# Sixteen-head attention of a two-layer decoder: on even quads the shifted scores are transposed before the exponential, and the norm's last scaling is done by GpSimd

## The reference, cut to what matters

```python
x = _layernorm(x + _L1_attn_ref(x, ...))           # 16 heads, band mask
x = _layernorm(x + _L1_xattn_ref(x, ctx, ctx, ...)) # 16 heads, no mask

scores = einsum('bhqd,bhkd->bhqk', qh, kh) * scale  # 16 heads of 16
attn = softmax(scores, axis=-1)
out = einsum('bhqk,bhkd->bhqd', attn, vh)
concat = out.transpose(0, 2, 1, 3).reshape(B, LQ, D_MODEL)
return concat @ Wo + bo
```

## Time and profile before

| | us |
|---|---|
| median of 3 runs | 1810.71 |
| lowest, highest | 1802.79, 1812.08 |
| the profiled execution | 1797.77 |
| its span, first to last instruction | 1795.9 |

### The profile page before, as it was taken

How to read it: one execution, slowest core, us unless ns; L and a number is a source line. 1 busy time by engine, 2 the same in 40 slices (tenths; PEclk the granted TensorE clock), 3 DMA queues, 4 the chain that set the end, 5 groups by cost and what they waited for, 6 DMA issues and landing times.

```text
span 1795.9 us, 28713 instructions
## 1 busy us (share of the span) xinstructions
PE 1699.1 (95%) x10847; PEld 1507.1 (84%) x10896; DVE 1058.9 (59%) x2330; ACT 624.3 (35%) x1459; POOL 113.1 (6%) x105
## 2 busy tenths in 40 slices
PE   6999999998999999989999879999998999999997
PEld 5888888887989998977777669999998888989896
DVE  6766676675555544575555456677676364444446
ACT  0312222132222222212222245566665334444443
POOL 1000000000000000020000023111111000000001
PEclk9999999998999999989999979999898899999999
DMA  5000000101111111100000185565662000010001
GB/s 200 1 22 4 13 12 12 35 1 46 36 34 36 34 35 33 33 9 18 13 29 0 17 117 67 73 81 78 100 85 46 25 12 25 13 29 18 23 23 47
DMA packets 43778, 68.98 MB, mean 38 GB/s; under 512 B 4640, under 2 KB 33568, under 8 KB 43552
## 3 DMA queue, kind: packets, MB, share of 16 engines
q1 hardware_dynamic: 43680, 67.71, 19.1%
HBM read 36.24 MB, written 2.10 MB: 21 GB/s over the span
## 4 chain that ended last, share of the span: by engine, by line
PE 85%; DVE 9%; issue 3%; ACT 1%; DMA 1%; SPq 1%; DVEq 0%; POOL 0%; POOLq 0%; ACTq 0%
PE ps L111 22%; PE ps L112 21%; PE ps L113 21%; PE ps L1591 6%; PE ps L411 3%; PE ps L1578 3%; PE ps L430 2%; PE ps L1568 2%; PE ps L419 1%; PE ps L440 1%; PE ps L1117 1%; DVE X L917 1%; SPq L1426 1%; DVE a1PT L617 1%; PE ps L1601 1%
## 5 line engine op out<-in xcount | busy, mean ns | idle before, releaser
L898 DVE TENSOR_TENSOR m6hT_l<-m6h,m6hT_h 128x512 fp32r<-128x512 f32 x128 | 88.8, 694 | 189.8 <-ACT m6hT_h L804 189.6
L900 DVE SCALAR_TENSOR_TENSOR m2hT_l<-ps,m2hT_h 128x512 fp32r<-128x512 f32 x128 | 88.5, 691 | 157.5 <-ACT m2hT_h L806 157.5
L806 ACT ACTIVATE m2hT_h<-ps 128x512 fp32r<-128x512 f32 x128 | 76.4, 597 | 282.4 <-PE ps L113 282.4
L1673 ACT ACTIVATE nPr<-ps,negm 128x128 f32<-128x128 f32 x512 | 145.7, 370 | 66.4 <-DVE negm L1755 66.2
L803 ACT ACTIVATE m6h<-ps,m6b 128x512 f32<-128x512 f32 x128 | 88.2, 689 | 220.0 <-PE ps L113 205.3
L495 ACT ACTIVATE a1Pr<-ps,negm 128x128 f32<-128x128 f32 x256 | 73.0, 368 | 259.8 <-DVE negm L559 259.8
L111 PE MATMUL ps<-w_h,m6hT_h 128*128 128x256 f32 x512 | 145.4, 284 | 1.4 <-DVE X L917 0.8
L112 PE MATMUL ps<-w_l,m6hT_h 128*128 128x256 f32 x512 | 145.7, 285 | 0.0
L113 PE MATMUL ps<-w_h,m6hT_l 128*128 128x256 f32 x512 | 145.7, 284 | 0.0
L1755 DVE TENSOR_REDUCE negm<-ps 128x4 f32<-128x512 f32 x128 | 88.0, 688 | 97.4 <-PE ps L1568 97.3
L113 PE MATMUL ps<-m2w_h,m2hT_l 128*128 128x256 f32 x512 | 145.0, 283 | 0.0
(11 more groups left out here) (270 smaller groups left out, 4286.5 us busy)
## 6 DMA issues: line engine op xcount, KB each, us to landing
nKm<-nKc_h SPq DMA_DIRECT2D x64, 128.0 KB, 4.5
nQs<-nQc_h SPq DMA_DIRECT2D x64, 128.0 KB, 6.7
raw<-in_w_e1i SPq DMA_DIRECT2D x9, 512.0 KB, 3.5
raw<-in_w_e1o SPq DMA_DIRECT2D x9, 512.0 KB, 3.7
raw<-in_w_e6i SPq DMA_DIRECT2D x9, 512.0 KB, 3.6
raw<-in_w_e6o SPq DMA_DIRECT2D x9, 512.0 KB, 3.6
raw<-in_w_a SPq DMA_DIRECT2D x8, 512.0 KB, 4.2
nKm<-nKc_l SPq DMA_DIRECT2D x32, 128.0 KB, 5.2
```

The source lines that it names most:

```text
L806: nc.scalar.activation(c.hT[0][:, ch, :], ps[:, u % 2, :], ACT.Relu).then_inc(c.s["hi_ready"], 1)
L898: last = nc.vector.tensor_tensor(c.hT[1][:, ch, :], c.h32[:, u % 2, :], c.hT[0][:, ch, :].bitcast(F32), ALU.subtract)
L900: last = nc.vector.scalar_tensor_tensor(c.hT[1][:, ch, :], ps[:, u % 2, :], 0.0, c.hT[0][:, ch, :].bitcast(F32), ALU.max, ALU.subtract)
L1673: last = nc.scalar.activation(N.Pr[:, i % 4, j, :], ps[:, SB[i % 2], j * S:(j + 1) * S], ACT.Exp, bias=negm[:, i % 4, j:j + 1])
```

## The change

On even quads VectorE, as soon as it has the negated maximum, adds it to the four heads' scores in one instruction (`negm` broadcast along each head) and writes the result to `nPr`, signalling `p_even`. TensorE transposes these shifted scores, and ScalarE takes the exponential of the transposed bank in one instruction of 512 columns. On odd quads the exponential stays where it was (signal `p_odd`), and ScalarE copies the transposed bank as before. So ScalarE takes every transposed bank back to SBUF, and VectorE none; `pt_even` and `pt_odd` become one `pt_ready`. The normalised `X` is written by GpSimd right behind its power, and not by VectorE two steps later; the residual sum of sequence B waits until the `X` of sequence B - 2 is written. `following` comes after all of VectorE's steps.

```diff
     def pt_ready(n):
-        return N.s["pt_odd" if n % 2 else "pt_even"], n // 2 + 1
+    def p_ready(n):
+        return N.s["p_odd" if n % 2 else "p_even"], n // 2 + 1
...
-            steps += [(kind, (n - at) // 4) for kind, at in (("zn", 6), ("na", 9), ("ns", 9), ("nb", 11))
+            steps += [(kind, (n - at) // 4) for kind, at in (("zn", 6), ("na", 9), ("ns", 9))
...
                 nc.gpsimd.tensor_tensor(rstd[:, b:b + 1], veps[:, b:b + 1], mhalf[:, b:b + 1],
                                         ALU.pow).then_inc(s["rstd_ready"], 1)
+                pool.wait_ge(s["rstd_ready"], i + 1)
+                nc.gpsimd.tensor_scalar(X[:, i % B, :], N.r[:, i % 2, :], mv[:, b, 0:1], rstd[:, b:b + 1],
+                                        ALU.subtract, ALU.mult).then_inc(s["x_done"], 1)
...
             if n >= 2:
-                pe.wait_ge(s["p_ready"], n - 1)
+                pe.wait_ge(*p_ready(n - 2))
...
         def transpose_p(n):
-            pe.wait_ge(s["p_ready"], n + 1)
+            pe.wait_ge(*p_ready(n))
             if n > 1:
-                pe.wait_ge(*pt_ready(n - 2))
+                pe.wait_ge(s["pt_ready"], n - 1)
...
         def transposed_p(n):
             act.wait_ge(s["pt_full"], n + 1)
             nc.scalar.activation(N.PT[:, n % 2, :, :].rearrange("p a b -> p (a b)"), ps[:, TB[n % 2], :],
-                                 ACT.Identity).then_inc(s["pt_odd"], 1)
+                                 ACT.Identity if n % 2 else ACT.Exp).then_inc(s["pt_ready"], 1)
...
             elif kind == "s":
-                if i >= 2 and i % 2:
+                if i >= 2:
                     transposed_p(i - 2)
-                act.wait_ge(s["s_max"], i + 1)
-                for j in range(QH):
-                    last = nc.scalar.activation(N.Pr[:, i % 4, j, :], ps[:, SB[i % 2], j * S:(j + 1) * S], ACT.Exp,
-                                                bias=negm[:, i % 4, j:j + 1])
-                last.then_inc(s["p_ready"], 1)
+                if i % 2:
+                    act.wait_ge(s["s_max"], i + 1)
+                    for j in range(QH):
+                        last = nc.scalar.activation(N.Pr[:, i % 4, j, :], ps[:, SB[i % 2], j * S:(j + 1) * S], ACT.Exp,
+                                                    bias=negm[:, i % 4, j:j + 1])
+                    last.then_inc(s["p_odd"], 1)
...
         def norm_a(B):
+            if B >= 2:
+                v.wait_ge(s["x_done"], B - 1)
...
                 nc.vector.reduce_max(negm[:, i % 4, :], ps[:, SB[i % 2], :].rearrange("p (h k) -> p h k", h=QH), AX.X,
                                      negate=True).then_inc(s["s_max"], 1)
-            elif kind == "t":
                 if i % 2 == 0:
-                    v.wait_ge(s["pt_full"], i + 1)
-                    nc.vector.tensor_copy(N.PT[:, i % 2, :, :].rearrange("p a b -> p (a b)"), ps[:, TB[i % 2], :]).then_inc(s["pt_even"], 1)
+                    v.wait_ge(s["s_max"], i + 1)
+                    nc.vector.tensor_tensor(N.Pr[:, i % 4, :, :], ps[:, SB[i % 2], :].rearrange("p (h k) -> p h k", h=QH),
+                                            negm[:, i % 4, :].unsqueeze(2).broadcast_to([P, QH, S]), ALU.add).then_inc(s["p_even"], 1)
...
-            elif kind == "nb":
-                if i == NSEQS - 1:
-                    following()
-                norm_b(i)
+        following()
```

More of the change, by code:

```diff
@@ L1368, in program @@
     N.V, N.Km, N.Qs, N.XB = n_V, n_Km, n_Qs, n_XB
-    N.s = signals("n", "g_full g_evac xt_hi qk_hi ct_hi ct_ready ctx_loaded s_full s_max p_ready pt_full pt_even pt_odd z_full "
+    N.s = signals("n", "g_full g_evac xt_hi qk_hi ct_hi ct_ready ctx_loaded s_full s_max p_even p_odd pt_full pt_ready z_full "
                        "rec_done z_ready zt_full zt_hi zt_ready o_full r_done xb_ready ln_var rstd_ready x_done")
@@ L1372, in program @@
     N.k_laid = [sem(f"n_k_laid{j}") for j in range(2)]
-    def pt_ready(n):
-        return N.s["pt_odd" if n % 2 else "pt_even"], n // 2 + 1
+    def p_ready(n):
+        return N.s["p_odd" if n % 2 else "p_even"], n // 2 + 1
     SB = (0, 1)
@@ L1395, in n_order @@
             step = [("s", n), ("t", n - 2), ("pv", n - 3)]
-            step += [(kind, (n - at) // 4) for kind, at in (("zn", 6), ("zt", 7), ("o", 8), ("na", 8), ("ns", 9), ("nb", 10))
+            step += [(kind, (n - at) // 4) for kind, at in (("zn", 6), ("zt", 7), ("o", 8), ("na", 8), ("ns", 9))
                      if (n - at) % 4 == 0]
@@ L1587, in values @@
                     pe.wait_ge(s["z_ready"], n // 4)
-            pe.wait_ge(*pt_ready(n))
+            pe.wait_ge(s["pt_ready"], n + 1)
             for i in range(QH):
@@ L1665, in n_scalar @@
             elif kind == "t":
-                if i >= NQUADS - 2 and i % 2:
+                if i >= NQUADS - 2:
                     transposed_p(i)
             elif kind == "s":
-                if i >= 2 and i % 2:
+                if i >= 2:
                     transposed_p(i - 2)
-                act.wait_ge(s["s_max"], i + 1)
-                for j in range(QH):
-                    last = nc.scalar.activation(N.Pr[:, i % 4, j, :], ps[:, SB[i % 2], j * S:(j + 1) * S], ACT.Exp,
-                                                bias=negm[:, i % 4, j:j + 1])
-                last.then_inc(s["p_ready"], 1)
+                if i % 2:
[4 more added lines that the diff above has]
+                    last.then_inc(s["p_odd"], 1)
             elif kind == "zt":
@@ L1734, in norm_stats @@
             nc.vector.tensor_scalar(veps[:, b:b + 1], mv[:, b, 1:2], LN_EPS, None, ALU.add).then_inc(s["ln_var"], 1)
[L1736 to L1742, removed]
         for kind, i in n_order_vector():
```

## The result

The changed kernel takes 1855.22 us (median of 4 runs, 1846.89 to 1862.35), against 1811.07 for the kernel before: a ratio of 1.0252, 95% interval 1.0198 to 1.0307. That is 44 us slower, where 28 were forecast. The direction and the range held. The size did not hold in one term. Each kernel is measured beside runs of the kernel before on the same chip, and ratios and intervals leave out runs over 1.5% slower than the fastest of their kernel, which the medians keep.

The account below looks back on a forecast made before the run. TensorE, busy 95% of the span, was taken to bound the kernel. Output projection stops 17.8, longer `z_ready` stops 2.4 and lower clock 8 made 28 us, set on the median 1810.7: 1839 us, range 1820 to 1862.

Parts of the forecast that it names:

- Part 1: ScalarE's exponentials: one of 512 columns for four, taken as 600 ns, and the even copies; cost 0.
- Part 2: VectorE's subtraction ahead of `late`: `nzT_l` 0.71 us later, output projection stops 17.8 us, longer `z_ready` stops 2.4 us.
- The 2.4 us of that term: Chain to `z_ready` in step 4B+6: 0.12 us longer at each of 20 stops, bounds 0 and 4.8.
- Part 3: Norm's scaling moved from VectorE to GpSimd, at most 635 ns there: cost 0, bounds -0.5 and +1 us.
- Part 4: TensorE's clock after the added stops: four falls of 2.1 us net, 8 us, bounds 0 and 32.
- The bound of 32: Upper bound of the lower-clock cost on TensorE: 15 falls x 2.1 us.
- No clock term: Rival: TensorE's new stops cost only their length, no lower clock; 1831 us, chance 0.17.
- After every second stop: Rival: TensorE's clock falls after every second stop, 13 to 15 falls; 1861 us, chance 0.10.
- The stop doesn't form: Rival: `nzT_l` late before the output projection, but the change of step elsewhere covers it; 1813 us, chance 0.05.
- faster: Rival: VectorE, freed of copy and scaling, delivers `z_ready` in time; 1796 us, chance 0.03.

Follow-up runs that it names:

- the first experiments: Changed kernel with the subtraction moved behind `late`: 1812.74 us; kernel before with only `late` moved behind the copy: 1837.21 us.

## Why the prediction was right or wrong

**Part 1, ScalarE: right.** The exponential of 512 columns cost 0.60 us, the value taken, and no wait of TensorE in the run is put down to ScalarE.

**Part 2, the subtraction: right in its place and its size.** 1.33 us from the maximum to `nzT_l` against 1.32 forecast (by the prediction's own rows `nzT_l` is then 0.72 us later, not 0.71); 25 stops with 16.1 us against 26 with 17.8; 0.12 to 0.14 us more in most like stops at `z_ready`. The 2.4 us of that term did not show in the sum (13.2 us against 14.0), since there were no such stops at the lower clock and three others were shorter. The two kernels with only the order changed, one in each direction, show that this place is the cause of the stops and of the whole loss in the changed kernel.

**Part 3, the scaling: right in cost, wrong in price.** It cost nothing, but GpSimd takes 1.23 us, not at most 0.64. The row it was bounded by has one operation on two tensors; this one has two operations with a value of each partition, and no row of before had that on GpSimd. A row of before that the prediction doesn't use points the other way: GpSimd's one operation with a constant took longer than that subtraction of the same shape, so 635 ns was no upper bound.

```profile
L683 POOL TENSOR_SCALAR raw<-raw 128x512 f32<-128x512 f32 x1 | 1.6, 1584 | 0.0
```

**Part 4, the clock: the step that failed.** I wrote 8 us, 4 falls of 2.1 us net. The profiled executions show 41 us more lost; on the medians, 44 less the 15 us of stops, it is about 29. The error was to count each fall as an event of its own with the mean cost of the seven falls before. A fall in the last group is not such an event: it lasted 75 us there, against 48 with the subtraction behind `late`, and these 27 us at half the clock, 13 us of work, are by themselves more than the whole term. The other falls, too, took more time than three or four of the old ones: against the same kernel 30 us of work went in all. The bound of 32 was right for the medians. Why a stop of 0.7 us is followed by a fall in one place and not in another stays open. The mean granted clock of the 13 runs of the kernel before that share a chip with the first experiments is 0.947 to 0.956; the profiled execution had 0.960, so its 1797.8 us and its 39 us at the lower level were those of a lucky run, and the spell was out of its sight. That the range held owes something to its width, which came from rivals with another mechanism.

The rule that only idle gaps of several microseconds cost clock (Trainium skill, "TensorE: Matmul & The Clock Gate", "HAM oscillation — how this bites in real kernels") gave a term of 0. The order of one instruction on VectorE, with no stop longer than 1.21 us at these places up to 1430 us in the changed kernel, moved the clock from 0.91 to 0.84. This case does not bear the rule out.

**The rivals.** "No clock term" gave 1831, below every run. "After every second stop" gave 1861, nearer than my own value though not by its own mechanism. "The stop doesn't form" and "faster" both fell with the first timeline: no work elsewhere covers it, and `z_ready` came later.

## What to carry to other kernels

Where an engine works through a hand-written queue, a moved instruction costs by what stands behind it: list for each what waits for it and by when, and put the one with the most room last. A swap that spares a slack engine was worth nothing here until it was used that way; swap and order together then gave 2%, and the order alone, with the copy, gave nothing. Price small stops of TensorE above their length: here 16 us of them brought some 30 us of lower clock, more for each stop in the second attention than in the first. Compare runs by their mean clock before comparing them by time, and take a profile whose time is near the median.

## What the runs showed of the hardware that was not expected

Behind stops of 0.7 us in the last groups came 71 to 75 us at the lower clock level, with TensorE over 90% busy, and 59 of these us in one profile without a gap; 14 such stops in the first half of the run left the clock at 0.98. With stops of at most 0.3 us it stayed at 1.00 for 286 us. Nine runs of one kernel on one chip differ by 18 us, in step with their mean clock.

GpSimd's subtract-and-multiply by two values of each partition took 1228 ns for 128x256 elements in fp32, where a subtraction of two tensors of twice the size takes 1272.
